# A three-layer decoder block on one core: one state's turn and output weights on GpSimd, the expert weights in two transfers, an engine order rewritten

## Chip, cores and metric

One core of a Trainium2 chip. The time is that of one execution in microseconds of device time; the figure is the median of three runs. Engines are named TensorE (PE in the profile, its weight load PEld), VectorE (DVE), ScalarE (ACT), GpSimd (POOL) and SyncE (SP, which issues the DMAs).

## What is computed

Four batches of 256 tokens with 256 features pass three layers, each followed by a residual add and a layer norm:

```
y   = 2*Re(C * scan(Lam_bar, B_bar u)) + D*u          # state space, 32 complex states
x1  = layernorm(x + y)
h   = quant(x1/s) @ quant(w*s).T * scales             # smoothed int8 product, w per batch
a   = silu(gate) * up                                 # gate, up = split(h)
x2  = layernorm(x1 + quant(a/s2) @ quant(dw*s2).T * scales2)
out = layernorm(x2 + sum over 8 experts of share_e * (silu(x2 G_e) * (x2 U_e)) P_e)   # top 2 of 8
```

The scan is kept real: the recurrence is turned into one with a real decay, and the states are turned back by tables of cosines and sines before they are multiplied by the output weights `cw1` and `cw2`. All eight experts are computed for all tokens (hidden size 8 x 176 = 1408, that is 11 chunks of 128); the shares of the experts that aren't chosen are 0.

## The kernel before

The work is written out by hand, engine by engine: each engine has small helper functions, one for a step, and then one list of calls with its whole order. Between engines there are semaphores, one for each kind of result. No planner decides anything at build time: the lists are the order.

- **SP** issues all loads in one list (lines 284 to 298): `par`, `bt`, `load_u(0)`, `d_raw`, `c1_raw`, `c2_raw`, `load_u(1)`, `load_expert(0)` (the weights `w_feat` and `dw_feat` of batch 0), `load_u(2)`, `load_u(3)`, then `gu_raw`, all the experts' first weights and the router's in one transfer of 2824 KB (semaphore `l_gu`), `load_expert(1)`, `dp_raw` (the second weights, 1408 KB, `l_dp`), and the rest. Later it copies each batch's shares of the experts out and back in, spread over the partitions (L263, L277).
- **The state** of batch b: `state_in(b)` (TensorE, L407), `state_scan(b)` (VectorE, L1371, L1372, in PSUM), `state_turn_c(b)` and `state_turn_s(b)` (VectorE, L1382, L1390: times cosine and sine), `state_out(b, t)` (TensorE: `residual` L414, L439, L440). The output weights are made in two parts: `cw1` by `output_scale` on GpSimd (L1138), `cw2` on ScalarE (L769), and then `output_weights(0)` and `(1)` on VectorE (L1343) add the second term. The sums of batch 0 lie in `ps_ab`, of batches 1 and 2 in the first bank of `ps_gu`.
- **The first norm**: statistics on VectorE (L1395, L1400), `rstd1(b)` on GpSimd (L1141 to L1145), `x1_norm` on ScalarE (L815), for batch 0 half on VectorE (L1405).
- **The quantized expert** of batch b: `x1_transpose`, `x_max` (L1410), `smooth_ratio` (L1417), `smoothing` (GpSimd, a power, L1158), `smooth_inverse` (L1423), `smooth_x` (L820) and `smooth_w` (L826) on ScalarE, `xs_transpose` and `ws_transpose` (L385), `quant_scales_x` and `quant_scales_w` (VectorE, L1430 to L1434: largest values, scales, reciprocals), `quant_x`, `quant_w` (L831, L836), transposes back, `unround` (L841, L1454), `expert_in` (L486), `gate_scale`, `up_scale`, `expert_silu`, `expert_act`, and the same once more with the second weights up to `expert_out` (L518), `expert_sum` (L1512), `rstd2` and `x2_norm`. Batch 0 has halves of these on VectorE (`..._first`).
- **Weights of the last layer**: ScalarE rounds them (`gate_up_hi(e)` for expert e, L775, two copies of 128x352; `down_hi(g)`, L784), GpSimd makes the remainders (`gate_up_lo(e, c)`, L1171; `down_lo(g)`).
- **The last layer**: `gate_up(b, p, kind)` (TensorE, L351 to L356; `p` a pair of chunks, 6 a batch; kind 0 gate, 1 up), `silu` (ScalarE, L792), `gated` (VectorE, L1575), `share_product` (GpSimd, L1185), `hid_hi_copy` (ScalarE, L811), `hid_lo_sub` (VectorE, L1581), `down(b, t, p)` (TensorE, L372 to L376), `moe_add` and statistics, `rstd3` (GpSimd), `moe_norm` (ScalarE, L911), `store`. The gate and up products turn through three banks:

```
def bank_of(b, p, kind):
    return ((b * NP + p) * 2 + kind) % BANKS
```

A `gate_up` waits for the bank's reader three products before (`act_up_ready` or `sil_ready`). `keep_busy(bank, n)` (L531) are filler matmuls on a matrix of ones; they compute nothing that is used. They stand in the first third of TensorE's list.

## Time and profile before

| | |
|---|---|
| median of 3 runs | 161.77 us (161.57 to 161.86) |
| the profiled execution, its own time | 162.29 us |
| its span, first to last instruction | 160.5 us |
| mean granted TensorE clock | 0.985 |
| busy TensorE / VectorE / ScalarE / GpSimd | 146.4 / 111.2 / 86.9 / 81.0 us |
| moved by DMA | 14.55 MB |

The profile has the busy time of each engine; the chain of waits, which goes back from the last instruction to what released each; timelines of an engine, with the idle time before an instruction and its releaser in brackets; and busy times by stretches. PEclk is the granted clock as a share of full speed. Some matmuls appear as two records (a product of fp32 data is two passes). Neighbours of one form are merged into one row (`x4`), whose time is from the first start to the last end.

### The profile page before, as it was taken

The page shows a single profiled execution, that of the slowest core. Times are in us where ns is not written, and L with a number is a line of the kernel's source. Part 1 is how long each engine was busy: PE and PEld are TensorE (multiplying, and loading weights), DVE is VectorE, ACT ScalarE, POOL GpSimd, SP SyncE. Part 2 cuts the span into 40 slices and gives each one's busy share as a digit, 9 for nine tenths or more (in the row PEclk, how much of TensorE's full clock was granted, in tenths as well). Part 3 has the DMA queues.
Part 4 walks back from the last instruction along what each step waited for, and adds up shares of the span by engine and source line. Part 5 has one row for each costly group of instructions (what it writes and reads, how often), then busy time and mean ns, then how long its engine had stood idle before and what let it go on. Part 6 is the DMA issues. An engine that isn't in the chain of part 4 may idle for free.

```text
span 160.5 us, 3397 instructions
## 1 busy us (share of the span) xinstructions
PE 146.4 (91%) x1158; PEld 139.7 (87%) x1158; DVE 111.2 (69%) x385; ACT 86.9 (54%) x187; POOL 81.0 (50%) x131
## 2 busy tenths in 40 slices
...
GB/s 104 263 383 422 354 325 22 0 0 0 6 0 4 87 150 121 7 0 4 66 154 146 35 0 33 6 30 158 135 111 0 0 55 122 159 62 6 33 0 65
DMA packets 13313, 14.55 MB, mean 91 GB/s; under 512 B 1744, under 2 KB 13040, under 8 KB 13040
## 3 DMA queue, kind: packets, MB, share of 16 engines
...
q8 instruction: 9, 0.15, 0.4%
...
## 4 chain that ended last, share of the span: by engine, by line
PE 75%; DMA 7%; DVE 6%; ACT 3%; SPq 3%; issue 2%; POOL 1%; POOLq 0%; ACTq 0%
PE ps_gu L351 13%; PE ps_gu L356 13%; PE ps_gu L352 13%; DMA gu_raw<-in_guT 7%; PE ps_out L372 6%; PE ps_out L376 6%; PE ps_out L373 6%; PE ps_ab L385 3%; PE ps_ab L390 2%; PE ps_s L385 2%; ACT gu_hi L775 1%; PE ps_gu L407 1%; PE ps_ab L486 1%; SPq L255 1%; PE ps_tr L322 1%
## 5 line engine op out<-in xcount | busy, mean ns | idle before, releaser
L351 PE MATMUL ps_gu<-x_hi,gu_hi 128*128 128x256 f32 x176 | 46.5, 286 | 0.0
L352 PE MATMUL ps_gu<-x_hi,gu_lo 128*128 128x256 f32 x176 | 45.6, 281 | 0.0
L1185 POOL TENSOR_TENSOR gu_raw<-gu_raw 128x512 f32<-128x512 f32 (+1 forms) x24 | 28.5, 1196 | 22.2 <-DVE gu_raw L1575 14.8
L356 PE MATMUL ps_gu<-x_lo,gu_hi 128*128 128x256 f32 x176 | 35.2, 282 | 0.0
L351 PEld LDWEIGHTS ps_gu<-x_hi,gu_hi 128*128 128x128 f32 x176 | 33.1, 188 | 0.1
L352 PEld LDWEIGHTS ps_gu<-x_hi,gu_lo 128*128 128x128 f32 x176 | 33.2, 188 | 0.0
L356 PEld LDWEIGHTS ps_gu<-x_lo,gu_hi 128*128 128x128 f32 x176 | 27.0, 188 | 0.0
L1581 DVE TENSOR_TENSOR hid_lo<-gu_raw,hid_hi 128x512 fp32r<-128x512 f32 (+1 forms) x24 | 15.0, 636 | 13.8 <-ACT hid_hi L811 13.8
L811 ACT ACTIVATE hid_hi<-gu_raw 128x512 fp32r<-128x512 f32 (+1 forms) x24 | 14.2, 594 | 13.0 <-POOL gu_raw L1185 12.8
L372 PE MATMUL ps_out<-dp_hi,hid_hi 128*128 128x256 f32 x77 | 20.4, 286 | 0.0
L1575 DVE TENSOR_TENSOR gu_raw<-sil,ps_gu 128x512 f32<-128x512 f32 (+1 forms) x24 | 15.2, 636 | 6.8 <-PE ps_gu L356 4.6
L373 PE MATMUL ps_out<-dp_lo,hid_hi 128*128 128x256 f32 x77 | 19.8, 278 | 0.0
L792 ACT ACTIVATE sil<-ps_gu 128x512 f32<-128x512 f32 (+1 forms) x24 | 13.5, 561 | 10.1 <-PE ps_gu L356 10.0
L376 PE MATMUL ps_out<-dp_hi,hid_lo 128*128 128x256 f32 x77 | 15.7, 278 | 0.0
L1171 POOL TENSOR_TENSOR gu_lo<-gu_raw,gu_hi 128x352 fp32r<-128x352 f32 x16 | 14.5, 932 | 1.4 <-ACT gu_hi L775 1.4
L373 PEld LDWEIGHTS ps_out<-dp_lo,hid_hi 128*128 128x128 f32 x77 | 14.5, 189 | 0.0
L372 PEld LDWEIGHTS ps_out<-dp_hi,hid_hi 128*128 128x128 f32 x77 | 14.5, 188 | 0.0
L376 PEld LDWEIGHTS ps_out<-dp_hi,hid_lo 128*128 128x128 f32 x77 | 11.9, 188 | 0.0
L1190 POOL TENSOR_TENSOR rs<-mv,ln_eps 128x1 f32<-128x1 f32 x7 | 1.7, 241 | 19.4 <-DVE mv L1594 19.2
L531 PE MATMUL ps_gu<-ones 128*128 128x128 f32 x54 | 8.8, 321 | 1.3 <-POOL ones L1094 1.3
L531 PEld LDWEIGHTS ps_gu<-ones 128*128 128x128 f32 x54 | 8.2, 233 | 1.3 <-POOL ones L1094 1.3
L911 ACT ACTIVATE u_feat<-u_feat,rs 128x256 f32<-128x256 f32 x7 | 4.2, 601 | 7.8 <-POOL rs L1192 7.6
...
## 6 DMA issues: line engine op xcount, KB each, us to landing
gu_raw<-in_guT SPq DMA_DIRECT2D x1, 2824.0 KB, 12.0
...
dp_raw<-in_dpT SPq DMA_DIRECT2D x1, 1408.0 KB, 15.3
...
```

The costliest lines, as they stand in the source:

```text
L351: pe.matmul(dst, gu_hi[:, c, kind, col], x2_hi[:, b % 2, c], start=(c == 0), stop=False)
L352: pe.matmul(dst, gu_lo[:, c, kind, col], x2_hi[:, b % 2, c], start=False, stop=False)
L356: last = pe.matmul(dst, gu_hi[:, c, kind, col], x2_lo[:, b % 2, c], start=False, stop=(c == DC - 1))
L372: pe.matmul(dst, hid_hi[:, h, tok], dp_hi[:, h], start=(h == 0), stop=False)
L373: pe.matmul(dst, hid_hi[:, h, tok], dp_lo[:, h], start=False, stop=False)
L376: last = pe.matmul(dst, hid_lo[:, h, tok], dp_hi[:, h], start=False, stop=(h == HC - 1))
L531: pe.matmul(bank[:, 0:P], ones[:], ones[:], start=True, stop=True)
L811: act.activation(hid_hi[:, lo:hi], hid[:, lo:hi], ACT.Copy).then_inc(hid_hi_ready, 1)
L1171: pool.tensor_tensor(gu_lo[:, c, :, col], gu_raw[:, c, E + e * GU:E + (e + 1) * GU].rearrange("p (k h) -> p k h", k=2), gu_hi[:, c, :, col ...
L1185: pool.tensor_tensor(hid[:, lo:hi], hid[:, lo:hi], shares[:, lo:hi], ALU.mult).then_inc(hid_ready, 1)
L1575: dve.tensor_tensor(hid[:, lo:hi], sil[:, n % 2, 0:hi - lo], split(ps_gu[:, bank_of(b, p, 1)])[:, 0:hi - lo], ALU.mult).then_inc(act_up_re ...
L1581: dve.tensor_tensor(hid_lo[:, lo:hi], hid[:, lo:hi], hid_hi[:, lo:hi], ALU.subtract).then_inc(hid_lo_ready, 1)
```

## The change

- **Weights.** `gu_raw` comes in two transfers by columns, 1416 (router and experts 0 to 3, `l_gu`) and 1408 (experts 4 to 7, `l_gu2`). The first goes out ahead of `load_u(2)`, the second behind it; `load_u(3)` goes behind `dp_raw`.
- **Batch 1's state** is scanned from PSUM into `z1` (the memory of `c1_raw`, free once both output scales are made), and GpSimd turns it. "Batch 1" is the second batch.
- **Output weights**: the sum for the cosines' (`cw1`) is made on GpSimd by a scaling and an addition; the sines' stays on VectorE.
- **Batch 0's quantizing scales** of inputs and weights are made by one function, with all four scales and both reciprocals at the end.
- **Banks**: the products start at the second bank, so the first bank, in which batch 2's sums lie, is used by the third product, and the wait for batch 2's norms moved there.
- **Order**: all five lists are written anew. TensorE has 31 fillers where it had 39.

```diff
 def bank_of(b, p, kind):
-    return ((b * NP + p) * 2 + kind) % BANKS
+    return ((b * NP + p) * 2 + kind + 1) % BANKS
...
+        z1 = c1_raw
...
             load_expert(0)
+            half, all_gu = E + E // 2 * GU, guT.rearrange("(c p) m -> p c m", p=P)
+            sp.dma_start(gu_raw[:, :, 0:half], all_gu[:, :, 0:half]).then_inc(l_gu, 16)
             load_u(2)
-            load_u(3)
-            sp.dma_start(gu_raw[:], guT.rearrange("(c p) m -> p c m", p=P)).then_inc(l_gu, 16)
+            sp.dma_start(gu_raw[:, :, half:], all_gu[:, :, half:]).then_inc(l_gu2, 16)
             load_expert(1)
             sp.dma_start(dp_raw[:], dpT.rearrange("(c p) m -> p c m", p=P)).then_inc(l_dp, 16)
+            load_u(3)
...
-                if b == 0 and first:
+                if n == BANKS - 1:
                     pe.wait_ge(x1_ready, halves(2))
...
             def state_out(b, t):
-                pe.wait_ge(zc_ready, b + 1)
-                pe.wait_ge(zs_ready, b + 1)
+                if b == 1:
+                    pe.wait_ge(zc1_ready, 1)
+                    pe.wait_ge(zs1_ready, 1)
+                else:
+                    pe.wait_ge(zc_ready, b)
+                    pe.wait_ge(zs_ready, b)
...
             state_in(0)
+            residual_first(0)
             state_in(1)
-            residual_first(0)
             residual_first(1)
...
             def gate_up_hi(e):
-                if e == 0:
-                    act.wait_ge(l_gu, 16)
+                if e % (E // 2) == 0:
+                    act.wait_ge(l_gu if e == 0 else l_gu2, 16)
...
+            def output_weights_c():
+                then(pool.tensor_scalar(zc[:, 1], c2_raw[:], column(25), 1.0, ALU.mult, ALU.mult))
+                pool.wait_ge(ct1_ready, 1)
+                pool.tensor_tensor(cw1[:], cw1[:], zc[:, 1], ALU.add).then_inc(cw1_ready, 1)
+            def state_turn_c():
+                pool.wait_ge(z_ready, 2)
+                pool.wait_ge(cw1_ready, 1)
+                pool.tensor_tensor(zc[:, 1], z1[:], cos_t[:], ALU.mult).then_inc(zc1_ready, 1)
+            def state_turn_s():
+                pool.wait_ge(z_ready, 2)
+                pool.tensor_tensor(zs[:, 1], z1[:], sin_t[:], ALU.mult).then_inc(zs1_ready, 1)
...
+                if b == 1:
+                    dve.wait_ge(ct1_ready, 1)
+                    dve.wait_ge(ct2_ready, 1)
+                    z = z1[:]
                 dve.tensor_tensor_scan(z, sv[:, 7:8].broadcast_to([P, S]), v, 0.0, ALU.mult,
                                        ALU.add).then_inc(z_ready, 1)
...
+            def quant_scales_first():
+                dve.wait_ge(xsT_done, 1)
+                dve.tensor_reduce(qmax[:, 0:2], ps_q_both[0], AX.X, ALU.max, apply_absolute_value=True)
+                dve.wait_ge(wsT_done, 1)
+                then(dve.tensor_reduce(qmax[:, 2:4], ps_w_both[0], AX.X, ALU.max, apply_absolute_value=True))
+                for i in range(4):
+                    last = dve.tensor_scalar(qsc[:, i:i + 1], qmax[:, i:i + 1], Q_EPS, 1.0 / QMAX, ALU.max, ALU.mult)
+                then(last)
+                dve.reciprocal(qinv[:, 0:2], qsc[:, 0:2]).then_inc(qsx_ready, 1)
+                dve.reciprocal(qinv[:, 2:4], qsc[:, 2:4]).then_inc(qsw_ready, 1)
...
-            state_turn_c(0)
-            output_weights(0)
-            output_weights(1)
             state_turn_s(0)
+            state_turn_c(0)
+            output_weights_s()
             state_scan(1)
             state_statistics(0, 0)
             state_statistics(0, 1)
-            state_turn_c(1)
             state_aggregate(0)
-            state_turn_s(1)
...
             weight_max(1)
-            quant_scales_x(0)
-            quant_scales_w(0)
+            quant_scales_first()
```

How the lists move, at three places. ScalarE in the head, before, from the sines' table (L760) on; `tokens` is `x1_norm`, `gu_hi` `gate_up_hi`, `xs` and `ws` the scaled inputs and weights, `dp_hi` `down_hi`:

```order
L760 ACTIVATE sin_t<-scratch 128x256
L815 ACTIVATE tokens<-ps_ab,rs 128x256
L775 ACTIVATE gu_hi<-gu_raw 128x2x176 x2
L764 ACTIVATE router_w<-gu_raw 128x2x8
L775 ACTIVATE gu_hi<-gu_raw 128x2x176 x4
L820 ACTIVATE xs<-ps_gu,smooth 128x256
L826 ACTIVATE ws<-w_feat,smooth 128x256 x2
L775 ACTIVATE gu_hi<-gu_raw 128x2x176 x2
L815 ACTIVATE tokens<-ps_gu,rs 128x256 x2
L831 ACTIVATE xq_r<-ps_ab,round_bias,qinv 128x256
L853 ACTIVATE scale_rows<-ps_s 128x256
L836 ACTIVATE wq_r<-ps_gu,round_bias,qinv 128x256
```

And now (its L769 is the sines' table):

```order
L769 ACTIVATE sin_t<-scratch 128x256
L784 ACTIVATE gu_hi<-gu_raw 128x2x176 x6
L824 ACTIVATE tokens<-ps_ab,rs 128x256
L773 ACTIVATE router_w<-gu_raw 128x2x8
L784 ACTIVATE gu_hi<-gu_raw 128x2x176 x4
L829 ACTIVATE xs<-ps_gu,smooth 128x256
L835 ACTIVATE ws<-w_feat,smooth 128x256 x2
L784 ACTIVATE gu_hi<-gu_raw 128x2x176 x2
L824 ACTIVATE tokens<-ps_gu,rs 128x256 x2
L793 ACTIVATE dp_hi<-dp_raw 128x1024
L845 ACTIVATE wq_r<-ps_gu,round_bias,qinv 128x256
L840 ACTIVATE xq_r<-ps_ab,round_bias,qinv 128x256
```

Three experts' copies (x6) stand ahead of `x1_norm(0, 1)`, those of experts 3 and 4 ahead of `xs`, and `down_hi(0)` (L793) ahead of batch 0's quantizing, with `quant_w` (L845) the first of it.

GpSimd in the head, before, from `output_scale` on (`rs` is `rstd1(0)`, `smooth` is `smoothing(0)`):

```order
L1138 TENSOR_SCALAR cw<-c_raw,sv 128x256
L1141 TENSOR_TENSOR rs<-mv,ln_eps 128x2
L1142 TENSOR_TENSOR rs<-rs,minus_half 128x2
L1145 TENSOR_SCALAR rs<-mv,rs 128x1 x2
L1158 TENSOR_TENSOR smooth<-ratio,half 128x2
L1171 TENSOR_TENSOR gu_lo<-gu_raw,gu_hi 128x2x176
```

And now:

```order
L1147 TENSOR_SCALAR cw<-c_raw,sv 128x256
L1151 TENSOR_SCALAR zc<-c_raw,sv 128x256
L1153 TENSOR_TENSOR cw<-cw,zc 128x256
L1159 TENSOR_TENSOR zc<-c_raw,cos_t 128x256
L1163 TENSOR_TENSOR zs<-c_raw,sin_t 128x256
L1166 TENSOR_TENSOR rs<-mv,ln_eps 128x2
L1167 TENSOR_TENSOR rs<-rs,minus_half 128x2
L1170 TENSOR_SCALAR rs<-mv,rs 128x1 x2
L1196 TENSOR_TENSOR gu_lo<-gu_raw,gu_hi 128x2x176
L1191 TENSOR_TENSOR router_w<-gu_raw,router_w 128x2x8
L1196 TENSOR_TENSOR gu_lo<-gu_raw,gu_hi 128x2x176
L1183 TENSOR_TENSOR smooth<-ratio,half 128x2
```

The second to fifth rows are new. `smoothing(0)` stood ahead of the first copy's remainder (`gu_lo`) and now has two of them and the router's ahead of it.

ScalarE in the bulk, at batch 1's last layer, before, from `silu(1, 2)`, the first `sil`, to `moe_norm(0, 0)`, the `u_feat` (`adq` and `scale_rows` belong to batch 2's second product, `xs` and `xq_r` to batch 3's first):

```order
L792 ACTIVATE sil<-ps_gu 128x512
L885 ACTIVATE adq<-ps_ab,unround_bias 128x512
L820 ACTIVATE xs<-ps_s,smooth 128x256
L889 ACTIVATE scale_rows<-ps_ab 128x256
L831 ACTIVATE xq_r<-ps_s,round_bias,qinv 128x256 x2
L792 ACTIVATE sil<-ps_gu 128x512
L911 ACTIVATE u_feat<-u_feat,rs 128x256
```

And now, from `hid_hi_copy(1, 0)` to `silu(1, 3)`:

```order
L820 ACTIVATE hid_hi<-gu_raw 128x512
L920 ACTIVATE u_feat<-u_feat,rs 128x256
L801 ACTIVATE sil<-ps_gu 128x512
L820 ACTIVATE hid_hi<-gu_raw 128x512
L845 ACTIVATE wq_r<-ps_ab,round_bias,qinv 128x256
L840 ACTIVATE xq_r<-ps_s,round_bias,qinv 128x256 x2
L801 ACTIVATE sil<-ps_gu 128x512
```

`silu(1, 2)` (the first `sil` row now) stands behind `hid_hi_copy(1, 0)` and `moe_norm(0, 0)`. On GpSimd `rstd3(0, 0)`, which `moe_norm(0, 0)` waits for, moved behind `share_product(1, 0)` and `(1, 1)`.

## Rows read from the trace of the kernel before

**Rows 1.** The page: busy time, share of the span and instructions of each engine.
```profile
PE 146.4 (91%) x1158; PEld 139.7 (87%) x1158; DVE 111.2 (69%) x385; ACT 86.9 (54%) x187; POOL 81.0 (50%) x131
```
**Rows 2.** Busy us by stretches: length, engines (instructions), PEclk, DMA share, GB/s.
```profile
0.00:10.00 10.00, 6.96 (x32) 6.15 (x32) 6.95 (x43) 6.19 (x14) 5.59 (x24) 1.00 0.71 220
10.00:20.00 10.00, 7.26 (x44) 6.18 (x44) 9.38 (x37) 2.44 (x7) 3.05 (x7) 1.00 1.01 389
...
24.00:25.00 1.00, 1.00 (x3) 0.78 (x3) 0.71 (x2) 1.00 (x4) 1.00 (x2) 0.50 0.30 91
...
45.00:50.00 5.00, 5.00 (x45) 4.99 (x43) 4.34 (x23) 3.65 (x10) 2.60 (x4) 1.00 0.01 2
```
**Rows 3.** Chain of waits in the head: start us, us, what.
```profile
6.08 12.02 DMA gu_raw<-in_guT
...
23.65 2.03 PE ps_gu L407 x4
```
**Rows 4.** Timeline of ScalarE: start us, us, line, what, [idle before <- releaser].
```profile
14.75 0.56 ACT L815 ACTIVATE tokens<-ps_ab,rs 128x256 f32<-128x256 f32 x1 [5.09 <-POOL rs L1145]
...
18.12 0.88 ACT L775 ACTIVATE gu_hi<-gu_raw 128x352 fp32r<-128x352 f32 x2 [2.81 <-DMA gu_raw<-in_guT]
...
19.02 1.64 ACT L775 ACTIVATE gu_hi<-gu_raw 128x352 fp32r<-128x352 f32 x4
```
**Rows 5.** `dp_raw`: its issue on SP, and from the DMA table us to landing.
```profile
8.07 0.43 SPq L296 DMA_DIRECT2D dp_raw<-in_dpT  x1
...
dp_raw<-in_dpT SPq DMA_DIRECT2D x1, 1408.0 KB, 15.3
```
**Rows 6.** GpSimd and VectorE in the head; `L1185` over the run: ns min/median/max.
```profile
8.43 0.48 POOL L1138 TENSOR_SCALAR cw<-c_raw,sv 128x256 f32<-128x256 f32 x1
...
13.19 0.39 DVE L1390 TENSOR_TENSOR zs<-ps_gu,sin_t 128x256 f32<-128x256 f32 x1
13.35 0.19 POOL L1141 TENSOR_TENSOR rs<-mv,ln_eps 128x2 f32<-128x2 f32 x1 [4.44 <-DVE mv L1400]
...
21.49 7.17 POOL L1171 TENSOR_TENSOR gu_lo<-gu_raw,gu_hi 128x352 fp32r<-128x352 f32 x8
...
L1185 POOL TENSOR_TENSOR gu_raw<-gu_raw x24: 718/1288/1300, 56.4 to 151.4; 128x512 f32<-128x512 f32 x20, 128x256 f32<-128x256 f32 x4
```
**Rows 7.** Timeline of the head at the points where the path passes.
```profile
7.37 1.13 PE L407 MATMUL ps_gu<-u_feat,bt 128*128 128x256 f32 x4 [1.17 <-DMA u_feat<-in_xT]
...
18.08 0.17 DVE L1423 RECIPROCAL smooth<-smooth 128x2 f32<-128x2 f32 x1
...
18.89 0.69 DVE L1347 TENSOR_REDUCE amax_w<-w_feat 128x2 f32<-128x512 f32 x1
...
21.07 0.66 PE L385 MATMUL ps_ab<-ident,xs 128*128 128x128 f32 x4 [2.84 <-ACT xs L820]
...
22.73 0.17 DVE L1434 RECIPROCAL qinv<-qsc 128x2 f32<-128x2 f32 x1
...
27.70 0.61 PE L486 MATMUL ps_ab<-xq,wq 128*128 128x256 bf16 x4 [0.26 <-ACT xq L841]
...
36.86 0.88 DVE L1512 SCALAR_TENSOR_TENSOR ps_ab<-ps_ab,qsc,scale_rows 128x256 f32<-128x256 f32 x2
...
43.09 0.39 PE L351 MATMUL ps_gu<-x_hi,gu_hi 128*128 128x256 f32 x1
```
**Rows 8.** Timeline of GpSimd and ScalarE in the bulk, on the shares' path.
```profile
56.41 1.29 POOL L1185 TENSOR_TENSOR gu_raw<-gu_raw 128x512 f32<-128x512 f32 x1 [2.54 <-DMA gu_raw<-share_rows]
58.72 1.28 POOL L1185 TENSOR_TENSOR gu_raw<-gu_raw 128x512 f32<-128x512 f32 x1 [1.02 <-DMA gu_raw<-share_rows]
...
75.50 0.37 ACT L801 ACTIVATE c_raw<-ps_tr 8x256 f32<-8x256 f32 x1 [0.18 <-PE ps_tr L329]
...
83.41 0.19 POOL L1190 TENSOR_TENSOR rs<-mv,ln_eps 128x1 f32<-128x1 f32 x1 [5.51 <-DVE mv L1594]
```
**Rows 9.** Timeline of TensorE: its last matmul.
```profile
155.54 0.28 PE L376 MATMUL ps_ab<-dp_hi,hid_lo 128*128 128x256 f32 x1
```

More of the change, by code:

```diff
@@ L195, in decoder_block @@
         share_tokens = c1_raw[0:E]
+        z1 = c1_raw
         s3, y3 = u_feat[:, 1], u_feat[:, 0]
         st3, mv3, rs3 = sb("st3", [P, TT, 6]), sb("mv3", [P, TT, 2]), sb("rs3", [P, TT, 4])
-        l_par, l_bt, l_c, l_d, l_gu, l_dp = (sem(n) for n in ("l_par", "l_bt", "l_c", "l_d", "l_gu", "l_dp"))
+        l_par, l_bt, l_c, l_d, l_gu, l_gu2, l_dp = (
+            sem(n) for n in ("l_par", "l_bt", "l_c", "l_d", "l_gu", "l_gu2", "l_dp"))
         l_w, l_dw = [sem(f"l_w{b}") for b in range(B)], [sem(f"l_dw{b}") for b in range(B)]
@@ L590, in _ @@
             gate_up(0, 3, 0)
+            aq_transpose(1)
             scale2_broadcast(1)
-            aq_transpose(1)
+            xq_transpose(2)
             dq_transpose(1)
-            xq_transpose(2)
+            gate_up(0, 3, 1)
+            scale_broadcast(2)
             ws_transpose(2)
-            gate_up(0, 3, 1)
             expert_out(1)
-            scale_broadcast(2)
+            state_in(3)
             gate_up(0, 4, 0)
             gate_up(0, 4, 1)
-            state_in(3)
+            gate_up(0, 5, 0)
+            down(0, 0, 0)
+            gate_up(0, 5, 1)
+            down(0, 0, 1)
             wq_transpose(2)
-            gate_up(0, 5, 0)
-            gate_up(0, 5, 1)
             x2_transpose(1)
@@ L607, in _ @@
             state_out(3, 1)
+            expert_in(2)
             router(1)
-            expert_in(2)
             gate_up(1, 0, 0)
```

378 lines of the change are left out of this document (189 added, 189 removed).

## The prediction, made before the changed kernel ran

> **What bounds the kernel now.** I read the page's shares first, then the busy table by stretches, the chain of waits over the head, the timelines of ScalarE, VectorE and GpSimd there, and the timeline of the bulk. TensorE is busy 91% of the span [rows 1], but unevenly: from 43.09 us, where the first expert matmul of `gate_up` starts [rows 7], to 155.82 (155.54 + 0.28), where the last `down` ends [rows 9], it has no hole; the stretch 45:50 reads 5.00 of 5.00 [rows 2]. Those 112.7 us are throughput: 528 matmuls of `gate_up` and 264 of `down` at about 0.12 us from start to start are 93, and routers, transposes and the experts of batches 1 to 3 fill the rest to within half a us. Nothing is to be won there by order, only lost. The tail behind is a fixed chain. So the time is the head, plus 112.7, plus new stalls.
>
> In the head the chain goes through the 2824 KB transfer of the weights, 12.02 us [rows 3]. ScalarE sits idle 2.81 us for it [rows 4], then makes three experts' copies in one run before it scales `xs`, although the reciprocal it needs was there at 18.25 (18.08 + 0.17) [rows 7]. TensorE waits 2.84 us for that `xs` and starts at 21.07 [rows 7]. After this hole the granted clock falls to 0.50, that is 1.2 GHz [rows 2], and `state_in(2)` takes 2.03 us on the chain [rows 3], where the same form took 1.13 before the fall [rows 7].
>
> **The change, part by part.**
>
> *Weights in two transfers.* By 10 us 2.20 MB have moved (220 GB/s), then 0.389 MB a us [rows 2]. All that is issued up to the whole weight transfer is 4.86 MB, due at 16.8; it lands at 18.10 [rows 3], so a transfer lands about 1.3 us behind its bytes. The first half now has 2.89 MB up to its end: 11.8 + 1.3 = 13.1. The second: 4.60 MB, 16.1 + 1.3 = 17.4. `dp_raw` was issued at 8.07 and landed 15.3 later, 23.4 [rows 5]; `load_u(3)`, 0.26 MB, is no longer ahead of it, 0.7 to 0.8 us at that rate: 22.6. SP issues one DMA more (0.47) under transfers that are queued anyway: nothing.
>
> *ScalarE.* It runs three experts' copies, six of 0.41 (1.64 for four) [rows 4], before `x1_norm(0,1)`: 13.1 + 2.5 = 15.6, where it ran at 14.75. That is a loss of 0.85, the change's one cost in the head. From `x1_norm(0,1)` to the reciprocal took 3.5 us (14.75 to 18.25): now 19.1. ScalarE meanwhile makes experts 3 and 4 (the latter from 17.4, done 18.3) and is free. TensorE can transpose `xs` at 19.65 instead of 21.07: 1.4 won.
>
> *GpSimd's turn.* One scaling of 0.48 [rows 6] and three two-input passes over 128x256. The row for that form and size is 718 ns (the least of `L1185`) [rows 6]. GpSimd was idle 4.44 us from 8.91 to 13.35 [rows 6]. Weights `cw1`: 8.91 + 0.48 + 0.1 + 0.72 = 10.2, before VectorE has `zc` at 10.45, since it turns the sines first. The batch-1 scan ends near 12.0; two passes end at 13.45, against 13.58 on VectorE (13.19 + 0.39) [rows 6]. `rstd1(0)` is queued behind them: 13.5 for 13.35, hidden since ScalarE comes only at 15.6. VectorE loses 0.8 us of turns and one pass of weights, and `residual_first(0)` moved ahead of `state_in(1)` delays that to about 9.5, before VectorE takes it at 10.8. Sum: 0. Bounds: 0.15 lost to 0.15 won. The rule against it is in the Trainium skill, "GPSIMD Engine Reference", Engine selection: elementwise passes with two inputs belong on VectorE, GpSimd being about twice as slow. The rows agree on the ratio, 0.72 to 0.39. By the rule the chain would grow by 0.66 and the gain below would be 0.65; I take 0, by the idle row.
>
> *Scales made together.* VectorE now has `weight_max(1)` (first pass 0.69 from 18.89 [rows 7], 1.3 in all) behind `smooth_x_first`: 19.65 to 20.9. Then two reductions of 0.69, four small scales, two reciprocals: both scales are ready near 22.9. Before, the first was ready at 22.90 (22.73 + 0.17) [rows 7] and the weights' 1.05 later. So TensorE's earlier 1.4 is lost for the first scale and 1.0 is kept for the second.
>
> *TensorE's clock.* Its holes in 16:26 are now 0.5, 0.3 and 0.6 instead of 2.84, so the clock should hold; `state_in(2)` starts at 22.25, behind `x1_norm(1,1)`, and ends at 23.2 instead of 25.68.
>
> *`down_hi(0)`* moved ahead of batch 0's quantizing on ScalarE. It waits for `dp_raw`: 22.6 to 23.65. Queued behind are `quant_w`, `quant_x`, `rows_copy` (0.4 from start to start, to 25.0) and the two unroundings (to 25.9). `expert_in(0)` starts at 25.95 for 27.70 [rows 7]: 1.75 won. ScalarE comes to `down_hi(0)` at 22.2, so here `dp_raw` is what binds; half a us on the first half of the weights changes little either way.
>
> *To the first `gate_up`.* The order is kept apart from `quant_scales_x(1)` ahead of `unround_first(dq)`: `expert_out(0)` wins only 1.35, `expert_sum(0)` 1.5 (35.35 for 36.86 [rows 7]), as it had waited for VectorE. GpSimd's eight copies (7.17 [rows 6]) end before `smoothing2(0)` is asked for. `x2`, its transposes and copies follow 1.5 earlier: `gate_up(0,0,0)` at 41.6. Eight filler matmuls fewer stand in holes: 0. The banks' turn lets the first two `gate_up` run without batch 2's norms, done by 39.3: 0.
>
> *The bulk.* The same TensorE work. Where I followed it, other engines keep up with 0.1 to 0.6 us in hand: `state_out(3)`, `x1_transpose(3)`, `share_transpose(1)`. I charge 0.2. Bounds: 0.1 won, 1.5 lost. *The tail:* after `down(3,0,5)` 1.7 us of TensorE remain for 2.4; batch 3's first norm still ends in them: 0.
>
> Sum: -1.5 + 0.2 = -1.3. The profiled execution, 162.29, would be 161.0; it stands 0.52 above the median of 161.77, so the median comes to **160.5 us**.
>
> **The rivals.**
>
> *A, the transfers land later than their bytes say.* Each of three waits on ScalarE (`l_gu`, `l_gu2`, `l_dp`) stops all behind it. For it: 1.3 us of lag rests on one transfer. If `dp_raw` keeps its 23.4, 0.8 of the gain goes: 161.3. Against: its share of the bytes is the same but for `load_u(3)`. The Trainium skill, "DMA: Bandwidth & Descriptors", Queues, rings and completion order, says that each DMA engine has its own ring and completion is not first in, first out over the engines; by that such lags may vary. The trace agrees in that the lag exists.
>
> *B, the clock falls all the same.* Fillers are fewer, 2 for 4 at 12 us. The price is the 0.9 us that `state_in(2)` paid, or somewhat more: 161.5. Against: no hole near 2.84 is left.
>
> *C, slower: ScalarE stands in `moe_norm(0,0)` with `silu(1,2)` behind it.* GpSimd's `rstd3(0,0)` moved behind `share_product(1,0)` and `(1,1)`, and `moe_norm(0,0)` ahead of `silu(1,2)`. In batch 0 the first product started at 56.41, released by the shares' DMA [rows 8], the second 2.3 later. Batch 1's shares copy ran at 75.50 [rows 8], now about 1.7 earlier; products at 79.4 and 81.7, `rstd3` to 84.4 (it started at 83.41 [rows 8]), the norm to 85.1, `silu` to 85.7. TensorE needs it for `gate_up(1,3,1)`, whose bank it empties, at 86.0. Margin 0.3. If products come 2 us later than I count, the stall is 1.7, and 0.1 of other loss makes 162.3; it decides at a stall of 1.5. For: SP issues 18 transfers, each pair behind a wait. Against: I have no row where TensorE waited on this path.
>
> *D, many small stalls in the bulk, 1 us together:* 161.3. The order there is wholly rewritten; against is that it moves pieces by few places.
>
> **How the numbers follow.** Forecast 0.58, A 0.14, B 0.08, C 0.10, D 0.10. A change under 0.2% (0.32 us) can hardly be told from none. Forecast, A and nearly all of D are faster: 0.80. B lies within: 0.09. C is slower: 0.11. Low end: `dp_raw` 0.4 earlier and no stall, 159.9. The high end takes in A, B and D: 161.9. What it leaves out is C and some tenths on each side.
>
> **What would show it.** Right: ScalarE's first copy at 13.1, `x1_norm(0,1)` near 15.6, `xs` at 19.1, granted clock 1.00 in 22:26, `down_hi(0)` released by `dp_raw` near 22.6, `expert_in(0)` near 26, the first `gate_up` at 41.6, TensorE 5.00 of 5.00 from 45 on, the last matmul at 154.5. Wrong: a first half later than 14; a clock of 0.50 in the head; a first `gate_up` later than 42.5; or waits of TensorE for `sil` or `hid_hi` after 60 us.

## The result and the profile after

The changed kernel takes 162.9 us (median of 20 executions, 161.75 to 165.9) where the kernel before takes 161.32 in the same series: ratio 1.0085, 95% interval [1.0063, 1.0107]. A second series gave 1.0085 again (e0 below). So it is slower by 0.85%, where 160.5 us (159.9 to 161.9) was forecast. Medians here are over all executions; ratios leave out executions that ran over 1.5% above the fastest of their kernel. The first profile is of an execution 1.3 us over its kernel's median, the second of one 0.2 us under its own.

| | before | changed, first profile | changed, second profile |
|---|---|---|---|
| span, us | 160.5 | 162.4 | 160.8 |
| first `gate_up` | 43.09 | 41.80 | 41.67 |
| last matmul | 155.54 | 157.41 | 155.79 |
| between them ("the bulk") | 112.45 | 115.61 | 114.12 |
| TensorE's waits in the bulk | none | 2.9 | 1.7 |

Busy time, share of the span and instructions by engine, first profile after (before: [rows 1]):

```profile
PE 145.2 (89%) x1142; PEld 137.1 (84%) x1142; DVE 111.2 (68%) x382; ACT 87.1 (54%) x187; POOL 86.2 (53%) x135
```

GpSimd is 5.2 us busier, TensorE no more than before, in a span that is 1.9 us longer.

The head came nearly as forecast. First ScalarE, then TensorE of the first profile after, in the head (start us, us, engine, line, what, idle before and its releaser):

```profile
13.08 2.43 ACT L784 ACTIVATE gu_hi<-gu_raw 128x352 fp32r<-128x352 f32 x6 [3.42 <-DMA gu_raw<-in_guT]
...
17.98 0.88 ACT L784 ACTIVATE gu_hi<-gu_raw 128x352 fp32r<-128x352 f32 x2 [1.14 <-DMA gu_raw<-in_guT]
...
18.91 0.47 ACT L829 ACTIVATE xs<-ps_gu,smooth 128x256 f32<-128x256 f32 x1
...
23.25 1.06 ACT L793 ACTIVATE dp_hi<-dp_raw 128x1024 fp32r<-128x1024 f32 x1 [1.11 <-DMA dp_raw<-in_dpT]
24.21 0.55 ACT L845 ACTIVATE wq_r<-ps_gu,round_bias,qinv 128x256 f32<-128x256 f32 x1
```
```profile
19.49 0.66 PE L390 MATMUL ps_ab<-ident,xs 128*128 128x128 f32 x4 [0.61 <-DVE xs L1459]
...
22.29 1.10 PE L412 MATMUL ps_gu<-u_feat,bt 128*128 128x256 f32 x4 [0.73 <-ACT tokens L824]
...
41.80 0.38 PE L356 MATMUL ps_gu<-x_hi,gu_hi 128*128 128x256 f32 x1
```

The hole of 2.84 us before the transposes of `xs` [rows 7] is 0.61 us now, and `state_in(2)` takes 1.10 us for 2.03 [rows 3]. `dp_raw` holds ScalarE for 1.11 us, and quantizing starts behind it. The loss is in the bulk, where the kernel before has no hole. Here are TensorE's waits after 42 us in the first profile, and its busy time by stretches (the first pair is length and busy us, the number after POOL's is the granted clock):

```profile
PE ps_ab L390 <- ACT x L905: 1.8, 2, 1.4
PE ps_gu L356 <- ACT sil L801: 1.1, 1, 1.1
```
```profile
65.00:70.00 5.00, 4.61 (x35) 4.28 (x35) 3.77 (x9) 2.08 (x6) 2.00 (x2) 1.00 0.00 0
85.00:90.00 5.00, 3.86 (x33) 3.66 (x33) 4.72 (x13) 2.67 (x6) 2.90 (x5) 1.00 0.64 167
...
95.00:100.00 5.00, 3.61 (x33) 3.41 (x31) 1.96 (x5) 4.10 (x9) 1.89 (x6) 1.00 0.00 0
```

Three holes: 0.4 us at 65 and 1.4 us at 95, for the normed `x2` of batches 1 and 2 (`x2_norm`, L905), and 1.1 us at 88, for `silu(1,2)`. All three engines that feed them stand still at about 80 to 84 us. SyncE and GpSimd, then ScalarE, then VectorE of the same profile:

```profile
75.41 0.27 SPq L265 DMA_DIRECT2D share_rows<-c_raw  x1
78.79 8.65 SPq L279 DMA_DIRECT2D gu_raw<-share_rows  x18
```
```profile
82.71 1.28 POOL L1210 TENSOR_TENSOR gu_raw<-gu_raw 128x512 f32<-128x512 f32 x1 [5.84 <-DMA gu_raw<-share_rows]
84.41 1.29 POOL L1210 TENSOR_TENSOR gu_raw<-gu_raw 128x512 f32<-128x512 f32 x1 [0.42 <-DMA gu_raw<-share_rows]
85.66 0.64 POOL L1215 TENSOR_TENSOR rs<-mv,ln_eps 128x1 f32<-128x1 f32 x1
...
91.58 1.29 POOL L1210 TENSOR_TENSOR gu_raw<-gu_raw 128x512 f32<-128x512 f32 x1 [1.06 <-DVE gu_raw L1618]
92.83 0.64 POOL L1166 TENSOR_TENSOR rs<-mv,ln_eps 128x2 f32<-128x2 f32 x1
93.55 0.70 POOL L1167 TENSOR_TENSOR rs<-rs,minus_half 128x2 f32<-128x2 f32 x1
94.35 1.08 POOL L1170 TENSOR_SCALAR rs<-mv,rs 128x1 f32<-128x1 f32 x2
```
```profile
84.02 0.63 ACT L820 ACTIVATE hid_hi<-gu_raw 128x512 fp32r<-128x512 f32 x1 [2.61 <-POOL gu_raw L1210]
87.33 0.60 ACT L920 ACTIVATE u_feat<-u_feat,rs 128x256 f32<-128x256 f32 x1 [2.67 <-POOL rs L1217]
87.83 0.58 ACT L801 ACTIVATE sil<-ps_gu 128x512 f32<-128x512 f32 x1
...
95.47 1.02 ACT L905 ACTIVATE x<-ps_ab,rs 128x256 f32<-128x256 f32 x2 [1.93 <-POOL rs L1170]
```
```profile
84.69 1.56 DVE L1624 TENSOR_TENSOR hid_lo<-gu_raw,hid_hi 128x512 fp32r<-128x512 f32 x1 [4.12 <-ACT hid_hi L820]
86.17 0.68 DVE L1462 TENSOR_REDUCE qmax<-ps_s 128x2 f32<-128x512 f32 x1
```

The first product of batch 1 starts at 82.71, 5.84 us idle, for a shares' DMA. ScalarE stands behind it in `hid_hi_copy(1,0)` and `moe_norm(0,0)` (L920), with `silu(1,2)` at 87.83: rival C. VectorE stands 4.12 us in `hid_lo_sub(1,0)`, with batch 3's scales and the sum of batch 2 behind it; the prediction did not see that. Two more things stand out. The pass at 84.69 takes 1.56 us, where the form's mean is 0.68. And in `rstd2(2)` (from 92.83) GpSimd's first operation takes 0.64 and the last two 1.08; in other places 0.20 and 0.50.

### The profile page after: what moved, and what is told of

It is laid out like the page before. It is cut to its first block, busy times and chain, and to the rows that moved or that the text cites. A ratio compares the mean times of both kernels' runs of the same rounds, so it can differ in the third digit from the quotient of the medians.

```text
span 162.4 us, 3371 instructions
## 1 busy us (share of the span) xinstructions
PE 145.2 (89%) x1142; PEld 137.1 (84%) x1142; DVE 111.2 (68%) x382; ACT 87.1 (54%) x187; POOL 86.2 (53%) x135
## 3 DMA queue, kind: packets, MB, share of 16 engines
HBM read 13.25 MB, written 1.08 MB: 88 GB/s over the span
## 4 chain that ended last, share of the span: by engine, by line
PE 50%; DMA 16%; SPq 8%; POOL 8%; ACT 7%; DVE 5%; issue 4%; POOLq 0%; ACTq 0%; DVEq 0%
PE ps_gu L356 9%; PE ps_gu L357 9%; PE ps_gu L361 9%; DMA dp_raw<-in_dpT 9%; DMA gu_raw<-share_rows 4%; PE ps_out L377 4%; PE ps_out L381 4%; PE ps_out L378 4%; SPq L279 4%; POOL gu_raw L1210 3%; DMA share_rows<-c_raw 3%; POOL rs L1170 1%; PE ps_ab L390 1%; ACT x L905 1%; POOL rs L1167 1%
## 5 line engine op out<-in xcount | busy, mean ns | idle before, releaser
L1624 DVE TENSOR_TENSOR hid_lo<-gu_raw,hid_hi 128x512 fp32r<-128x512 f32 (+1 forms) x24 | 15.9, 682 | 12.2 <-ACT hid_hi L820 12.2
L784 ACT ACTIVATE gu_hi<-gu_raw 128x352 fp32r<-128x352 f32 x16 | 6.7, 482 | 4.6 <-DMA gu_raw<-in_guT 4.6
L1215 POOL TENSOR_TENSOR rs<-mv,ln_eps 128x1 f32<-128x1 f32 x7 | 2.5, 354 | 12.5 <-DVE mv L1637 12.5
L920 ACT ACTIVATE u_feat<-u_feat,rs 128x256 f32<-128x256 f32 x7 | 4.2, 598 | 9.0 <-POOL rs L1217 9.0
L540 PE MATMUL ps_gu<-ones 128*128 128x128 f32 x42 | 7.7, 335 | 1.0 <-POOL ones L1103 1.0
```

The lines of the kernel that those rows point to most:

```text
L1624: dve.tensor_tensor(hid_lo[:, lo:hi], hid[:, lo:hi], hid_hi[:, lo:hi], ALU.subtract).then_inc(hid_lo_ready, 1)
```

## The experiments

Each kernel is the changed one unless said otherwise; the lines are calls in the engines' lists. A ratio is to the kernel before in the same series, with its 95% interval. The other columns are of one profiled execution; "waits" is TensorE's idle time in the bulk for other engines.

| | kernel | ratio | first `gate_up` | bulk, us | waits, us |
|---|---|---|---|---|---|
| e0 | the change again | 1.0085 [1.0054, 1.0116] | 41.67 | 114.12 | 1.7 |
| e1 | new head, old bulk | 0.9951 [0.9918, 0.9984] | 41.78 | 112.14 | none |
| e2 | old head, new bulk | 1.0165 [1.0103, 1.0228] | 43.91 | 114.86 | 2.0 |
| e3 | `silu`, `rstd3` put back | 1.0137 [1.0078, 1.0195] | 41.91 | 114.79 | 2.2 |
| e4 | `hid_lo_sub(1,0)` put back | 1.0013 [0.9975, 1.0051] | 42.29 | 113.62 | 1.0 |
| e5 | e3 and e4 | 0.9988 [0.9956, 1.0020] | 43.03 | 113.15 | 0.6 |
| e6 | e5, subtractions of batch 0 later | 1.0086 [1.0044, 1.0129] | 42.09 | 118.72 | 3.6 |
| e7 | before, with the loads and ScalarE's head | 1.0030 [0.9992, 1.0069] | 42.63 | 112.37 | none |
| e8 | e5, batch 2's norm freed | 1.0002 [0.9966, 1.0037] | 42.73 | 112.74 | 0.4 |
| e9 | e5, both norms freed | 0.9978 [0.9943, 1.0013] | 42.30 | 112.93 | 0.5 |
| e10 | before, with the loads and all head orders | 0.9969 [0.9934, 1.0004] | 41.90 | 112.31 | none |
| e11 | e1, two subtractions beside `rstd2(1)` | 1.0022 [0.9990, 1.0053] | 42.91 | 113.04 | 0.6 |
| e12 | both norms freed, nothing else | 1.0018 [0.9980, 1.0056] | 42.16 | 114.72 | 2.0 |
| e13 | e1 again | 0.9931 [0.9897, 0.9965] | 42.37 | 111.97 | none |
| e14 | e1, `down_hi` later | 0.9879 [0.9829, 0.9929] | 42.26 | 112.07 | none |
| e15 | e14 again | 0.9901 [0.9871, 0.9931] | 41.00 | 111.98 | none |
| e16 | e14, fillers in the first hole | 0.9887 [0.9842, 0.9933] | 42.42 | 111.98 | none |

The first `gate_up` is of one profiled execution and moves by over a us between executions of one order (e1 and e13, e14 and e15), the bulk by 0.2 us or less in those pairs. In the changed kernel it moved by 1.5 us (115.61 and 114.12), and the profiled executions of e6 and e12 took 4.2 and 1.5 us more than their kernels' medians. So a kernel with waits is judged by its ratio, and the profile shows where it waits.

### Where the loss is: e0, e1, e2

e1 takes each engine's list up to the first `gate_up` from the changed kernel (TensorE 45 calls, ScalarE 49, VectorE 56, GpSimd 39) and the rest from the kernel before; e2 the other way round.

e0: 

> The changed kernel, once more and unchanged, for a second profile. Theory 1 (the order): ScalarE and GpSimd reach moe_norm(0,0) late whatever the shares' transfer does; ratio 1.0085 again, TensorE's stall for sil near 88 us of 1.0 to 1.3 and for x2 of batch 2 near 95 of 1.3 to 1.6. Theory 2 (the transfer): the 3.1 us from issue to landing of batch 1's share rows (1.0 in batch 0 and in the kernel before) was chance; if it is about 1.0 in this profile, the products of batch 1 start near 80.5 instead of 82.71, the stall near 88 is under 0.3 us, and runs of this kernel spread over 1.5 us or more.

e1: 

> Everything of the change up to the first gate_up (weights in two transfers, GpSimd's turn, scales together, orders of the head, the banks' turn), and from there on the order of the kernel before on TensorE, ScalarE, VectorE and GpSimd. If the loss sits in the bulk's order alone (theories 1 and 3): the head's 1.3 us stay, 0.992 (0.990 to 0.995) of the kernel before. If starting the bulk 1.3 us earlier is itself the trouble (a transfer or an engine that does not come earlier by as much, rival theory 4): 0.998 to 1.005, with new holes of TensorE in 60:100.

e2: 

> The kernel before up to the first gate_up, and from there the changed order. If the loss sits in the bulk's order alone: the loss without the head's gain, 1.3 us behind the changed kernel, 1.016 (1.013 to 1.019), first gate_up at 43.1, holes for x2 and sil as in the changed kernel. If it takes the early start to bring the loss (theory 4): 1.000 to 1.005.

The loss is in the bulk's order alone: 162.75 us for e0 against 160.71 for e1, 2.0 us, and without the new head it is there too, 1.0165 for e2. Starting the bulk earlier costs nothing (e1 has no hole). Theory 2 holds in part: in e0 SyncE's next transfer, which waits for the share rows, went out 2.02 us behind theirs instead of 3.38 (75.41 to 78.79 above), and the hole at 88 is gone; but that for `x2` stays, 1.3 us, and so does the ratio. In e2 the rows came in 1.30 us and the bulk still took 114.86; its hole for `sil`, 0.70 us, was at 50.5, not at 88.

### Rival C alone: e3

```
ScalarE:  + silu(1, 2)      ahead of hid_hi_copy(1, 0), moe_norm(0, 0)
          - silu(1, 2)      behind them
GpSimd:   + rstd3(0, 0)     ahead of share_product(1, 0)
          - rstd3(0, 0)     behind share_product(1, 1)
```

> The changed kernel with two lines of its order put back: ScalarE does silu(1,2) ahead of hid_hi_copy(1,0) and moe_norm(0,0), GpSimd does rstd3(0,0) ahead of share_product(1,0). Theory 1 (rival C of the prediction, and its echo: gated(1,3) late, share_product(1,3) late, rstd2(2) late, x2 of batch 2 late): both stalls near 88 and 95 go, 2.2 to 2.7 us won on the changed kernel, ratio to the kernel before 0.993 (0.991 to 0.996). Theory 3 (rstd2 of batches 1 and 2 is late for reasons of its own: behind a product, and slowed beside VectorE's subtractions): only the 1.1 us near 88 go, the 0.4 near 65 and 1.2 or more near 95 stay, ratio 1.000 to 1.003.

Theory 1 falls: the ratio, 1.0137, is no better than 1.0085. `silu` is no longer waited for, but the norm of batch 2 is as late as ever (1.8 us of hole), since VectorE stands where it stood, e3's timeline of VectorE:

```profile
84.59 1.55 DVE L1624 TENSOR_TENSOR hid_lo<-gu_raw,hid_hi 128x512 fp32r<-128x512 f32 x1 [3.53 <-ACT hid_hi L820]
```

### VectorE in the same transfer: e4, e5

```
VectorE (e4, e5):  - hid_lo_sub(1, 0)   ahead of quant_scales_x(3)
                   + hid_lo_sub(1, 0)   behind expert_statistics(2)
ScalarE, GpSimd (e5): as in e3
```

e4: 

> The changed kernel with one line of VectorE's order put back: hid_lo_sub(1,0) behind expert_statistics(2), where it stood before. New theory 5: VectorE and ScalarE each stand in something that waits for batch 1's shares (VectorE in hid_lo_sub(1,0), 2.73 us idle; ScalarE in hid_hi_copy(1,0) and moe_norm(0,0)), with the scales and silu(1,2) of the chain to x2 of batch 2 behind it. Freeing VectorE alone leaves silu(1,2) at 86.3 and gated(1,2) behind it: ratio to the kernel before 1.0085 as the changed kernel (1.005 to 1.012), the hole before x2_transpose(2) still over 1 us. Rival theory 6 (VectorE alone holds the chain, ScalarE is harmless): 0.998 to 1.001 and no hole near 95.

e5: 

> The same with silu(1,2) and rstd3(0,0) put back as well (the norm behind silu): three instructions of 430 moved. Theory 5: gated(1,2) near 84.5, rstd2(2) near 90, x2_norm(2) near 92, no hole in 85:100; 1.3 to 1.8 us won on the changed kernel, ratio to the kernel before 0.996 to 0.999, with only the 0.4 us hole near 65 left. Theory 7 (many small displacements, none decisive): over 1.003.

In e4 VectorE no longer stands for the shares ahead of batch 3's scales:

```profile
81.78 0.69 DVE L1462 TENSOR_REDUCE qmax<-ps_s 128x2 f32<-128x512 f32 x1 [0.49 <-PE ps_s L390]
```

One line of VectorE's list gives back 0.7%: 1.0013 for 1.0085, intervals apart. That is about half of what the bulk's order costs, 1.3 to 1.5% (1.0085 against 0.9951 and 0.9931 for the new head with the old bulk, e1 and e13). My expectation for e4 was wrong, its rival (ScalarE harmless) nearer; two holes for `x2` are left, 0.4 us near 66 and 0.6 near 95. The two lines of e3 add little to it (0.9988, intervals overlap). In e5's profile the share rows came in 1.29 us, so it does not show what late rows would do there.

### What is left: the norms of x2, e8, e9, e12

In e5 VectorE has the sum of batch 2 at 88.2 but takes its statistics only behind `gated(1,3)`, whose matmuls the new TensorE order asks for later; e5's timeline of VectorE:

```profile
87.50 0.70 DVE L1558 TENSOR_TENSOR ps_ab<-ps_ab,tokens 128x512 f32<-128x512 f32 x1
90.19 0.69 DVE L1618 TENSOR_TENSOR gu_raw<-sil,ps_gu 128x512 f32<-128x512 f32 x1 [2.00 <-PE ps_gu L361]
90.80 0.76 DVE L1563 BATCH_NORM_STATS2 st<-ps_ab 128x6 f32<-128x256 f32 x2
```

```
VectorE:  gated(1, 3) behind expert_statistics(2)     e9, e12 also gated(0, 3) behind (1)
GpSimd:   rstd2(2) ahead of share_product(1, 3)       and rstd2(1) ahead of (0, 3)
ScalarE:  x2_norm(2) ahead of hid_hi_copy(1, 3)       and x2_norm(1) ahead of (0, 3)
e8, e9 on top of e5, e12 on top of the changed kernel
```

e8: 

> The kernel with three engines put back (ratio 0.9988), and batch 2's second norm freed of gate_up(1,3): VectorE does gated(1,3) behind expert_statistics(2) instead of ahead of it (it idled 2.00 us there, although the sum was there at 88.2), GpSimd does rstd2(2) ahead of share_product(1,3), ScalarE x2_norm(2) ahead of hid_hi_copy(1,3). Theory 9 (the chain to x2 of batch 2 stands behind gated(1,3), which the changed TensorE order asks for 4 us later): mv of batch 2 at 89 for 91.8, x2_norm(2) by 92, no hole in 85:100, 0.3 to 0.6 us won; the hole of 0.4 near 65 stays. Rival: the freed chain only moves the wait (silu(1,3) or share_product(1,3) late, a hole for hid_hi or sil after 95): no gain.

e9: 

> The same for batch 1 as well: gated(0,3) behind expert_statistics(1), rstd2(1) ahead of share_product(0,3), x2_norm(1) ahead of hid_hi_copy(0,3). Theory 9: x2_norm(1) starts near 62 for 64.25, no hole near 65; from the first gate_up to the last matmul 112.2 to 112.6 us as in the kernel before (112.45), ratio 0.990 to 0.996, the head's gain whole. If the changed TensorE order itself costs something that no other engine's order gives back: over 113, ratio over 0.997.

e12: 

> The changed kernel with nothing but the norms of x2 of batches 1 and 2 freed: VectorE does gated(b,3) behind expert_statistics(b+1), GpSimd rstd2(b+1) ahead of share_product(b,3), ScalarE x2_norm(b+1) ahead of hid_hi_copy(b,3), for b 0 and 1. silu(1,2), rstd3(0,0) and hid_lo_sub(1,0) stay where the change put them. If the norms alone carry the loss: no hole for x2 after 45 us, bulk 112.4 to 113.0, ratio 0.995 to 0.999. If the instructions that wait for batch 1's shares hold VectorE and ScalarE ahead of them: the hole near 65 goes, that near 95 is still 0.5 or more, and sil is waited for near 88 whenever the share rows land late; ratio 1.001 to 1.006.

The bulk falls to 112.74 in e8, and in e9 no wait for `x2` is left (the norms start at 63.81 and 90.62, 64.25 and 93.94 in e0). A wait of 0.5 us for `gated`, which is now the later one, takes its place in e9, so the bulk is 112.93, still 0.8 over e1's. In the ratios neither step is to be told from e5 (0.9988, 1.0002 and 0.9978). The rest to e1 and e13, 0.3 to 0.5% (the intervals overlap), belongs to TensorE's order, or to what the others owe it; it was not taken apart further. e12, the norms alone, comes to 1.0018, as far as e4 with its one line (1.0013). In its profile no hole for `x2` is left, but `sil` is waited for 1.1 us again, and VectorE stands for batch 1's shares as before:

```profile
85.26 1.72 DVE L1624 TENSOR_TENSOR hid_lo<-gu_raw,hid_hi 128x512 fp32r<-128x512 f32 x1 [3.92 <-ACT hid_hi L820]
```

So there is no one decisive line. Two different edits on the path to batch 2's norm, VectorE's subtraction moved behind (e4) and the norms moved ahead (e12), give back about half of the loss each; both together, with e3's lines, stand at 0.9978 (e9), an interval that overlaps with theirs.

### Who slows GpSimd's small operations: e6, e11

```
e6, TensorE:  down(0,0,0), down(0,0,1) from ahead of x2_transpose(1) to behind gate_up(1,0,1)
e6, VectorE:  hid_lo_sub(0,0), (0,1) from behind expert_statistics(1) to behind the turns of batch 3
e11, VectorE (of e1): hid_lo_sub(0,0), (0,1) to directly behind expert_statistics(1)
```

e6: 

> The same, and down(0,0,0), down(0,0,1) behind gate_up(1,0,1) with their hid_lo_sub(0,0), (0,1) behind the turns of batch 3, so that no subtraction of VectorE runs beside rstd2(1). If the first pass of rstd2(1) is slow because of VectorE's pass over two operands in SBUF: it takes 0.20 for 0.65 and the last two 0.50 for 1.00, x2_norm(1) starts 0.7 or more earlier, the 0.4 us hole near 65 goes and the ratio is 0.993 to 0.996. If it is slow for another reason: 0.65 and 1.00 stay and the hole too, no change from the experiment before.

e11: 

> The kernel with the new head and the old bulk (0.9951), and one thing moved: VectorE's hid_lo_sub(0,0) and (0,1), passes whose two operands are both in SBUF, directly behind expert_statistics(1), so that they run beside GpSimd's rstd2(1), whose operations are of 128x1 and 128x2. Theory 10 (a VectorE pass over two SBUF operands shuts GpSimd out while it runs): the operation that begins beside a pass grows from 0.20 to 0.6 or more, the pair at L1170 from 0.50 to 1.0 or so, rstd2(1) in all from 1.56 to 2.2 or more, x2_norm(1) later by as much; in the time 0 to 0.5 us lost, as that norm has about half a us in hand. Rival: GpSimd's operations were slow for another reason in the changed kernel: 0.20, 0.69 and 0.50 stay.

e6 got slower instead, 1.0086 for e5's 0.9988, intervals apart. Its profile, with 118.7 us of bulk, is of an execution 4.2 us over its kernel's median, so the sizes there are not the usual ones. Its first operation took 0.20 as expected, but the subtractions now ran beside the last two. `rstd2(1)` of GpSimd, and VectorE and TensorE, in e6:

```profile
62.74 0.20 POOL L1166 TENSOR_TENSOR rs<-mv,ln_eps 128x2 f32<-128x2 f32 x1
63.01 0.69 POOL L1167 TENSOR_TENSOR rs<-rs,minus_half 128x2 f32<-128x2 f32 x1
63.81 2.36 POOL L1170 TENSOR_SCALAR rs<-mv,rs 128x1 f32<-128x1 f32 x2
```
```profile
63.63 2.48 DVE L1624 TENSOR_TENSOR hid_lo<-gu_raw,hid_hi 128x512 fp32r<-128x512 f32 x4
```
```profile
67.28 1.12 PE L390 MATMUL ps_ab<-ident,x 128*128 128x128 f32 x4 [3.36 <-ACT x L905]
```

Two operations of 128 numbers took 2.36 us, 0.50 elsewhere, and ended when the last of four subtractions did (66.11). The norm behind them came late, TensorE stood 3.36 us, and its granted clock fell to 0.60 in 65:70. In e11, where only the place of two subtractions differs from e1, `rstd2(1)` was, beside VectorE's row:

```profile
61.63 0.55 POOL L1166 TENSOR_TENSOR rs<-mv,ln_eps 128x2 f32<-128x2 f32 x1 [0.47 <-DVE mv L1566]
62.25 1.02 POOL L1167 TENSOR_TENSOR rs<-rs,minus_half 128x2 f32<-128x2 f32 x1
63.37 0.50 POOL L1170 TENSOR_SCALAR rs<-mv,rs 128x1 f32<-128x1 f32 x2
```
```profile
61.47 1.26 DVE L1624 TENSOR_TENSOR hid_lo<-gu_raw,hid_hi 128x512 fp32r<-128x512 f32 x2
```

and in e1:

```profile
60.50 0.20 POOL L1166 TENSOR_TENSOR rs<-mv,ln_eps 128x2 f32<-128x2 f32 x1
60.77 0.69 POOL L1167 TENSOR_TENSOR rs<-rs,minus_half 128x2 f32<-128x2 f32 x1
61.56 0.50 POOL L1170 TENSOR_SCALAR rs<-mv,rs 128x1 f32<-128x1 f32 x2
```

So `rstd2(1)` takes 2.24 us with the subtractions beside it and 1.56 without (61.63 to 63.87; 60.50 to 62.06): theory 10 holds for the operations, though it is the middle operation that grew most (1.02 for 0.69), not the last. The Trainium skill, "SBUF — State Buffer", Who interferes with whom, says that VectorE with two SBUF inputs and GpSimd reading SBUF exclude each other for a whole instruction, whoever issues first. These runs agree (0.20 to 0.55 us and 0.69 to 1.02 in e11), and in e6's profile a run of four passes went with GpSimd's last two operations ending only with the last pass. What this alone costs in time is not shown: e11 is slower than e1, 1.0022 for 0.9951, more than the 0 to 0.5 us expected, but TensorE waited there for `gated` and for `zs`, the sines' turn of batch 3 (0.3 us each), which VectorE makes behind the moved subtractions, and not for `x2`.

### The head's parts: e7, e10

```
e7 (on the kernel before):  the two transfers and the loads' order; ScalarE's list up to unround_w(1)
e10: and TensorE's and VectorE's new order up to the first gate_up
     (no turn and no weights on GpSimd, scales one after the other, banks as before)
```

e7: 

> The kernel before with the two transfers, their place among the loads and ScalarE's new order up to unround_w(1), and nothing else: VectorE turns batch 1 and makes the scales one after the other, GpSimd's list, TensorE's list and the banks as before. By the prediction's sum the GpSimd turn is worth 0 and the head's gain comes from the transfers: first gate_up near 41.8, ratio 0.993 (0.990 to 0.997). Rival: without the turn on GpSimd and state_in(2) ahead of the scales' broadcast the gain is lost to VectorE: first gate_up over 42.5, ratio over 0.997.

e10: 

> The kernel before with the transfers and with the new order of the head on all engines (TensorE, ScalarE, VectorE up to the first gate_up), but without GpSimd's turn and cosine weights, without the scales made together, and with the banks as before. The loads with ScalarE's order alone gave a first gate_up at 42.63 and 1.003: there xq was transposed first while ScalarE now made wq first. If those pieces are worth 0, as the prediction's sum has it, and the pairing of the orders is what was missing: first gate_up 41.7 to 42.0, ratio as with the whole new head, 0.9951 (0.991 to 0.998). If the GpSimd turn or the joint scales carry gain: first gate_up over 42.3.

In e7 `dp_hi(0)` starts at 23.20, where it started at 23.25 in the first profile, but ScalarE now makes `wq_r` first and TensorE still transposes `xq_r` first, so `expert_in(0)` starts at 27.24 instead of 26.49. With the orders paired (e10) the head is there. GpSimd's turn, its weights, the joint scales and the banks' turn are the difference between e10 (41.90, 0.9969) and e1 and e13 (41.78 and 42.37, 0.9951 and 0.9931): not to be told from 0, which is what the sum had, though up to 0.4% would not show either.

### What binds the head: e13 to e16

```
ScalarE (e14 to e16):  - down_hi(0)   ahead of quant_w(0, 0)
                       + down_hi(0)   where down_hi(1) was;  (1) where (2) was;  (2) behind unround_w(1)
TensorE (e16):         + keep_busy(ps_gu[:, 2], 4)   behind state_in(0)
```

e13: 

> The new head with the old bulk, a second time, unchanged. If its gain is real: 0.9951 again, between 0.992 and 0.998; the bulk 112.1 to 112.4 us, whatever the loads do to the start of it (41.7 to 43.0).

e14: 

> The new head with the old bulk, and ScalarE's three down_hi moved one place back: down_hi(0) behind batch 0's unroundings, down_hi(1) where (2) was, (2) behind unround_w(1). If dp_raw binds the head: ScalarE makes wq_r at 22.9 instead of 24.2 and TensorE transposes it at 24.1 instead of 24.8, right behind state_in(2); VectorE's scan of batch 2 is next, so expert_in(0) starts near 26.1 for 26.48 and the first gate_up near 41.4, and it no longer moves with dp_raw's landing; ratio 0.002 to 0.003 below its neighbour of this series. Rival (dp_raw does not bind, or VectorE's scan already does): no change, within 0.1 us.

e15: 

> New head, old bulk, down_hi one place back, a second time. If its gain over its neighbour without the move is real (0.9951 and 0.9931 for that one): 0.987 to 0.993. In a profile whose clock holds at 1.00 to 16 us: ScalarE's wq_r waits for no transfer, first gate_up near 41.4; with a clock of 0.50 in 8:12: near 42.2 as before.

e16: 

> The same with four filler matmuls (0.9 us) between state_in(0) and residual_first(0). If the hole there lets the clock fall: 1.00 in 8:12 and 12:16 in the profile, first gate_up 41.2 to 41.5, ratio 0.985 to 0.991, and a narrower spread than 159.7 to 161.1. Rival: the clock falls for another reason, or the fillers delay residual_first(0) (diag is there at 8.13): 0.50 again, or a ratio over its neighbour's.

Where `down_hi(0)` stands ahead of quantizing in the new head, `gate_up` follows it at a fixed distance: it starts at 23.13, 23.25, 24.20 in e0, the first profile and e8, and `gate_up` at 41.67, 41.80, 42.73, each 18.5 later. In eleven profiles ScalarE waited there for `dp_raw`, 0.4 to 1.5 us; in e4, e5 and e13, whose heads ran late from the start, it came too late to wait, at 23.74 to 24.43. Out of the way (e15), quantizing waits for VectorE only, its ScalarE row:

```profile
22.84 0.56 ACT L845 ACTIVATE wq_r<-ps_gu,round_bias,qinv 128x256 f32<-128x256 f32 x1 [0.30 <-DVE qinv L1477]
```

and the first `gate_up` is at 41.00. The gain, 0.9879 and 0.9901 against 0.9951 and 0.9931 without it, is more than the 0.002 to 0.003 expected; the intervals of e13 and e14 overlap, as do those of e1 and e15, and the profiles of e13 and e14, both with a clock of 0.50 at 8 us, have the first `gate_up` at 42.37 and 42.26. So its size is open. e14 to e16 are the fastest kernels of this study, 1.0 to 1.2% below the kernel before.

The first hole explains part of the scatter. Here are e13 and e1, the row behind the hole of TensorE and the stretch behind that:

```profile
8.26 1.19 PE L419 MATMUL ps_ab<-diag,u_feat 128*128 128x128 f32 x4 [2.57 <-DVE diag L1336]
```
```profile
8.00:12.00 4.00, 3.74 (x13) 3.41 (x14) 3.16 (x8) 1.77 (x5) 2.14 (x5) 0.50 0.95 350
```
```profile
8.13 0.68 PE L419 MATMUL ps_ab<-diag,u_feat 128*128 128x128 f32 x4 [1.75 <-DVE diag L1336]
```
```profile
8.00:12.00 4.00, 3.40 (x19) 2.99 (x20) 3.31 (x7) 1.64 (x5) 2.01 (x5) 1.00 0.91 340
```

In eight profiles (e4 to e8, e13 to e15) that hole was 2.19 to 2.57 us and the granted clock in 8:12 0.50 to 0.63, 1.2 GHz for part or all of it; in the eleven others it was 1.10 to 1.85 and the clock 1.00. How long the fall lasts counts: e13 and e14 have 0.72 and 0.73 in 12:16 as well, e15 has 1.00 there and the earliest `gate_up` of all. The reordered residual is not needed for it: e7 has TensorE's old order and stood 2.45 us for `u_feat`, with 0.62 behind. e16's fillers shortened it to 1.40 and the clock held, but there the first half of the weights landed at 14.42, the clock fell in 16:24 (0.81, 0.77), and the first `gate_up` was at 42.42. Its median is that of e15 (160.10 and 160.26), so a gain of the fillers is not shown.

## Why the prediction was wrong

**The head, -1.5.** Mechanism right, size a little off. Its profiles with a clock of 1.00 won 1.29 and 1.42 us; over executions, e1 and e13 won 0.5 and 0.7%, 0.8 to 1.1 us. Two things fit the rest. One is the landing: 13.1 us for the first half of the weights is the earliest of what came (13.08 to 14.49 in the profiles), and `dp_raw` came at 23.1 to 24.4, not 22.6 (where ScalarE waited for it). That is rival A: up to 1.4 us late on the first, 0.5 to 1.8 on the second. The other is the clock, below.

**GpSimd's turn, joint scales, banks: 0.** Nothing speaks against it (e10). "Here `dp_raw` is what binds" held in eleven of the fourteen profiles with that order; e14 and e15, without `down_hi(0)` ahead of quantizing, are 0.3 to 0.7% faster than e1 and e13, with intervals that overlap.

**TensorE's clock.** `state_in(2)` took its 1.10. But rival B's fall came in some executions, and at another place, at 8 us, where `residual_first(0)` now waits for `diag` (in e7 `state_in` for `u_feat`); I had looked at the holes in 16:26 only.

**The bulk, +0.2 (bounds 0.1 won, 1.5 lost).** This is the step that failed: it cost 2.0 us by medians (e0 against e1), 1.7 and 3.2 in the two profiles. "Where I followed it, other engines keep up with 0.1 to 0.6 us in hand" named `state_out(3)`, `x1_transpose(3)` and `share_transpose(1)`, and none of those was late. Not followed were the second norms of batches 1 and 2, and what VectorE stands in on the way to them. What held TensorE up instead was `x2` of batches 1 and 2, 1.7 to 1.8 us in the two profiles, and `sil` with 1.1 in one of them. The upper bound, 1.5, had no working behind it.

**Rival C (0.10).** Its place, its mechanism and its sign came true in the first profile, with 1.1 us of stall; yet putting its lines back alone won nothing (e3), and e0's profile has no such stall although its bulk is 1.7 us too long. The wait that cost time was its twin on VectorE (e4), for the same transfer, on the way to a norm that the new order also placed late (e12). That it came true in the first profile was in part luck: e0, the same kernel, did not have it. A margin of 0.3 us on a path with 18 DMAs in it deserved more than a tenth.

**The tail, 0.** Right: 4.99 us from the last matmul to the end of the span, 4.96 before.
